# Spectral products by even and odd halves of the DFT tables, inside the projection's program, and attention's first stacks loaded early

## The reference, cut to what matters

```python
# x: (2, 8192, 512); 16 heads of 32; window W = 64
h   = layernorm(x)
qkv = h @ w_qkv                                  # 512 -> 1536
out_local  = softmax over the keys from 32 before to 31 after each query, times v
out_global = softmax over every 64th key, times v
x = x + layernorm((out_local + out_global) @ w_out + b_out)
# spectral layer, w = w_freq_real + i*w_freq_imag, (512, 512)
y = real(ifft(fft(layernorm(x)) @ w)) + bias     # both over the last axis, 512
x = x + layernorm(y)
```

## Time and profile before

| | |
|---|---|
| median of 3 runs | 3774.73 us (3774.47 to 3777.2) |
| the profiled execution | 3778.02 us, of which the span is 3775.7 us |
| PE busy | 3697.7 us (98%) |
| DVE, POOL, ACT busy | 2319.9, 1928.3, 1587.6 us |
| projection, in the trace | start to 1125.5 us |
| spectral products | 1137.0 to 1223.6 us |
| attention | 1225.5 us to the end |

### The profile page before, as it was taken

The page is one execution under the profiler, slowest core; times in us unless marked ns, Lnnn a source line. Parts: engine busy times, 40 slices in busy tenths (PEclk is TensorE's granted clock), DMA queues, the critical chain, the costliest instruction groups (busy, mean ns, idle before and its releaser), DMA issues.

```text
span 3775.7 us, 77146 instructions
## 1 busy us (share of the span) xinstructions
PE 3697.7 (98%) x28480; PEld 2682.5 (71%) x28480; DVE 2319.9 (61%) x5331; ACT 1587.6 (42%) x3094; POOL 1928.3 (51%) x3087
## 2 busy tenths in 40 slices
PE   8999999999999899999999999999999999999997
PEld 6888888888874566666666666666666666666675
DVE  4333333333323567777777777777777777777774
ACT  3222222222220344555555555555555555555554
POOL 0000000000000367777777777777777777777777
PEclk9999999999999899999999999999999999999999
DMA  4554455445556456666666666666666666666651
GB/s 154 191 200 169 165 200 191 166 176 200 184 204 155 96 129 152 151 140 142 144 148 145 139 148 153 151 140 141 144 149 145 139 149 149 152 140 140 144 119 40
DMA packets 421938, 574.34 MB, mean 152 GB/s; under 512 B 41688, under 2 KB 186216, under 8 KB 421624
## 3 DMA queue, kind: packets, MB, share of 16 engines
q1 hardware_dynamic: 413080, 567.94, 57.1%
q10 hardware_dynamic: 8256, 2.16, 0.2%
q0 software_dynamic: 288, 0.08, 0.0%
HBM read 364.74 MB, written 203.23 MB: 150 GB/s over the span
## 4 chain that ended last, share of the span: by engine, by line
PE 62%; POOL 1%; ACTq 1%; ACT 0%; DVE 0%; issue 0%; POOLq 0%
PE ps_misc L995 19%; PE ps_max L915 10%; PE ps_sc L935 6%; PE ps_o L967 6%; PE ps_max L918 5%; PE ps_s L967 4%; PE ps_sc L949 4%; PE ps_o L979 3%; PE ps_s L973 3%; PE ps_sc L1004 1%; ACTq L782 1%; PE ps_sc L924 1%; PE ps_sc L943 1%; ACT qk L759 0%; POOL rsb L696 0%
## 5 line engine op out<-in xcount | busy, mean ns | idle before, releaser
L827 DVE TENSOR_REDUCE mx<-ps_max 128x2 f32<-128x256 f32 (+1 forms) x1365 | 485.0, 355 | 489.8 <-PE ps_max L918 466.7
L759 ACT ACTIVATE qk<-ps_sc 128x384 f32<-128x384 f32 (+1 forms) x1024 | 418.9, 461 | 666.0 <-PE ps_sc L935 663.3
L828 DVE TENSOR_REDUCE mx<-ps_max 128x2 f32<-128x384 f32 (+1 forms) x1365 | 612.6, 449 | 0.0
L915 PE MATMUL ps_max<-ks,qs 97*128 97x384 f32 x2048 | 569.1, 357 | 15.1 <-DVE mx L828 13.1
L915 PEld LDWEIGHTS ps_max<-ks,qs 97*128 97x128 f32 x2048 | 368.6, 192 | 180.9 <-DVE mx L828 127.1
L705 POOL TENSOR_SCALAR_AFFINE_SELECT qk<-qk 128x512 f32<-128x512 f32 (+1 forms) x512 | 298.5, 583 | 282.6 <-ACT qk L759 282.5
L371 PE MATMUL po<-ht_hi,w_hi 128*128 128x512 f32 x1024 | 405.6, 396 | 1.5 <-ACT ht_hi L248 1.5
L371 PE MATMUL po<-ht_hi,w_lo 128*128 128x512 f32 x1024 | 400.3, 391 | 0.0
L371 PE MATMUL po<-ht_lo,w_hi 128*128 128x512 f32 x1024 | 399.8, 390 | 0.0
L772 ACT ACTIVATE v<-ps_sc 128x512 f32<-128x512 f32 x512 | 298.2, 596 | 152.4 <-PE ps_sc L949 150.2
L918 PE MATMUL ps_max<-mask,ident_b 128*128 128x192 bf16 x2048 | 352.9, 254 | 0.0
(11 more groups left out here) (114 smaller groups left out, 7507.5 us busy)
## 6 DMA issues: line engine op xcount, KB each, us to landing
ks<-k_hi_d SPq DMA_DIRECT2D x256, 288.0 KB
qs<-q_hi_d SPq DMA_DIRECT2D x256, 256.0 KB
ks<-k_lo_d SPq DMA_DIRECT2D x128, 288.0 KB
xb<-in_L_attn_x SPq DMA_DIRECT2D x132, 256.0 KB, 3.5
q_lo_d<-o_lo SPq DMA_DIRECT2D x32, 1024.0 KB, 8.7
k_lo_d<-o_lo SPq DMA_DIRECT2D x32, 1024.0 KB, 10.1
qs<-q_lo_d SPq DMA_DIRECT2D x128, 256.0 KB
vw<-v_d SPq DMA_DIRECT2D x128, 256.0 KB, 2.9
```

What stands on the lines that cost most here:

```text
L759: nc.scalar.activation(p_loc[:, i, 2 * hp:2 * hp + 2, lo:MW], ps_sc[n % 2][:, 0:2 * MW].rearrange("p (h n) -> p h n", h=2)[:, :, lo:MW], A ...
L827: nc.vector.tensor_reduce(mx[s % 2][:, 1, h:h + n, tile], ps_max[:, b:b + n, MW:MW + NGLOB], axis=AX.X, op=ALU.max)
L828: last = nc.vector.tensor_reduce(mx[s % 2][:, 0, h:h + n, tile], ps_max[:, b:b + n, 0:MW], axis=AX.X, op=ALU.max)
L915: nc.tensor.matmul(ps_max[:, b, 0:2 * MW], qs[g][0:ROWS_MAX, h, tile * P:(tile + 1) * P], both_keys(g, h, tile), start=True, stop=True)
```

## The change

The separate spectral program is gone: its work stands at the end of the projection's block, after each engine's last chunk. There is one barrier less.

The tables are two now, cos and sin, and each product uses only half of a table: 257 columns of cos (the part that is even in the column's index) and 255 of sin (the odd part). A tile needs 4 matmuls of 128x257 and 4 of 128x255, in two PSUM banks, where it had 8 of 128x512 in one. ACT copies the odd half out of PSUM, and DVE (`mirrored`) makes the full 512 columns with three instructions: left half as sum or difference, right half with reversed columns, and two single columns. The scale 1/512 is an ACT instruction on M instead of being in a table. The loop over tiles has steps 1 and 2 interleaved, on all 8 banks (`pt` and `po`).

The stacks lie in the projection's freed buffers (`w_both` is w_hi and w_lo in one; `low` is `o_lo0`). Groups 0 and 1 (`EARLY = 2`) are loaded in the first block, groups 2 and 3 at the start of attention, between the loads of the values. The memsets of groups 2 and 3's key rows go to POOL there. b_out and b_ffn are loaded in attention, w_out in the last chunk. `s_t` shares `r_glob`'s buffer. The mask and the bf16 identity are loaded at the program's start.

```diff
-    return np.stack([c, s, c / D, -s / D]).astype(np.float32)
+    return np.stack([np.cos(angle), np.sin(angle)]).astype(np.float32)
...
 # project_phase, sync: load_spectral, called ahead of the last chunk's stores
-                    sp.dma_start(v0[:], rows(dft_d[0])).then_inc(spec_loaded, 16)
-                    for k in range(2):
-                        sp.dma_start(qk0[:, k * KT:(k + 1) * KT, :].bitcast(F32), rows(dft_d[1 + k])).then_inc(spec_loaded, 16)
+                    sp.dma_start(cos, rows(dft_d[0])[:, :, 0:EVEN]).then_inc(spec_loaded[0], 16)
+                    sp.dma_start(sin, rows(dft_d[1])[:, :, 1:ODD + 1]).then_inc(spec_loaded[0], 16)
+                    sp.dma_start(wo, rows(w_out)).then_inc(spec_loaded[1], 16)
+                    sp.wait_ge(kg_copied, 2 * NCHUNK)
+                    sp.dma_start(kg_hi_d.rearrange("(a p) n -> p a n", p=P), kg_hi[:].bitcast(F32)).then_inc(kg_stored, 16)
+                    sp.dma_start(kg_lo_d.rearrange("(a p) n -> p a n", p=P), kg_lo[:].bitcast(F32)).then_inc(kg_stored, 16)
...
 # behind the last chunk's stores
+                sp.wait_ge(kg_stored, 32)
+                sp.wait_ge(pads, 16 * PADS)
+                for g in range(EARLY):
+                    sp.wait_ge(stacks.q_made, g + 1)
+                    sp.wait_ge(stacks.k_made[g], 2)
+                    stacks.load(sp, 0, g)
+                for u in range(2):
+                    sp.wait_ge(stored[u], 16 * 5 * NCHUNK // 2)
...
 # scalar
+                act.wait_ge(spec_loaded[1], 16)
+                for k in range(KT):
+                    nc.scalar.activation(wo_hi[:, k, :], wo[:, k, :], ACT.Copy).then_inc(split_hi, 1)
+                act.wait_ge(row_made, 1)
+                for n in range(2 * KT):
+                    act.wait_ge(spec_mm, n + 1)
+                    nc.scalar.activation(odd[n % 2][:, n // 2, :], banks[(2 * n + 1) % 8][:, 0:ODD], ACT.Copy).then_inc(odd_copied, 1)
+                    if n in (1, 4):
+                        act.wait_ge(stacks.k_made[n // 4], 2)
+                        stacks.load_ones(act, n // 4)
+                for a in range(KT):
+                    act.wait_ge(spec_mm, 2 * KT + a + 1)
+                    nc.scalar.activation(odd[0][:, a, :], banks[2 * a + 1][:, 0:ODD], ACT.Copy).then_inc(odd_copied, 1)
+                    act.wait_ge(m_sum, 3 * a + 3)
+                    nc.scalar.activation(wr[:, a, :], wi[:, a, :], ACT.Copy, scale=1.0 / D).then_inc(m_scaled, 1)
+                    act.wait_ge(m_scaled, a + 1)
+                    nc.scalar.activation(m_hi[:, a, :], wr[:, a, :], ACT.Copy).then_inc(split_hi, 1)
...
 # vector
+                def mirrored(dst, even, odd, sign, done):
+                    plus, minus = (ALU.add, ALU.subtract) if sign > 0 else (ALU.subtract, ALU.add)
+                    half = D // 2
+                    nc.vector.tensor_tensor(dst[:, 1:half], even[:, 1:half], odd, plus).then_inc(done, 1)
+                    nc.vector.tensor_tensor(dst[:, half + 1:D], even[:, half - 1:0:-1], odd[:, ::-1], minus).then_inc(done, 1)
+                    nc.vector.tensor_copy(dst[:, 0:half + 1:half], even[:, 0:half + 1:half]).then_inc(done, 1)
+
+                dve.wait_ge(mm_done, NCHUNK * (NOUT + TILES))
+                stacks.set_queries(nc, 0)
+                stacks.set_keys(nc.vector, 0)
+                for a in range(KT):
+                    for n, dst in ((2 * a, at), (2 * a + 1, bt)):
+                        dve.wait_ge(odd_copied, n + 1)
+                        mirrored(dst[:, a, :], banks[2 * n % 8], odd[n % 2][:, a, :], 1 if dst is at else -1, spec_sum)
+                    if a == 0:
+                        stacks.set_queries(nc, 1)
+                        stacks.set_keys(nc.vector, 1)
+                    if a in (1, 2):
+                        stacks.set_queries(nc, a + 1)
...
+                for a in range(KT):
+                    dve.wait_ge(odd_copied, 2 * KT + a + 1)
+                    mirrored(wi[:, a, :], banks[2 * a], odd[0][:, a, :], -1, m_sum)
+                    if a > 0:
+                        low(a - 1)
+                low(KT - 1)
...
 # tensor
+                pe.wait_ge(spec_loaded[0], 16 * 4)
+                pe.wait_ge(t_lo, NCHUNK * TILES)
+                pe.wait_ge(ev_dve, NCHUNK * NOUT)
+                for n in range(2 * KT):
+                    a = n // 2
+                    if n == 2:
+                        pe.wait_ge(ev_act, NCHUNK * (NOUT + TILES))
+                    at_least(pe, spec_sum, 3, n, -9)
+                    even, odds = ((wr, wi), (wi, wr))[n % 2]
+                    product(banks[2 * n % 8], even, cos, a)
+                    product(banks[(2 * n + 1) % 8], odds, sin, a).then_inc(spec_mm, 1)
+                pe.wait_ge(spec_sum, 6 * KT)
+                for a in range(KT):
+                    product(banks[2 * a], at, cos, a)
+                    product(banks[2 * a + 1], bt, sin, a).then_inc(spec_mm, 1)
...
 # attention, sync
-                for g in range(GROUPS):
-                    load_values(0, g)
+                load_values(0, 0)
+                for g in range(EARLY, GROUPS):
+                    sp.wait_ge(stacks.k_made[g], 2)
+                    stacks.load(sp, 0, g)
+                    load_values(0, g - 1)
+                load_values(0, GROUPS - 1)
```

More of the change, by code:

```diff
@@ L67, in dft, with project_phase @@
     angle = 2.0 * np.pi * ((n[:, None] * n[None, :]) % D) / D
[L68 to L73 removed]
+    return np.stack([np.cos(angle), np.sin(angle)]).astype(np.float32)
+def project_phase(nc, x, w_qkv, q_hi_d, q_lo_d, k_hi_d, k_lo_d, v_d, kg_hi_d, kg_lo_d, bias_d, ident_d, mask_d,
+                  w_real, w_imag, dft_d, w_out, common, stacks):
     NOUT = 2 * KT
@@ L84, in project_phase @@
         kg_lo = sb("kg_lo", [P, KT, BATCH * NGLOB], F32R)
[L85 to L88, removed]
+        at, bt = sb("at", [P, KT, D], F32), sb("bt", [P, KT, D], F32)
+        wr, wi = xb
+        cos, sin, wo = v0[:, :, 0:EVEN], qk0[:, 0:KT, 0:ODD].bitcast(F32), qk0[:, KT:2 * KT, :].bitcast(F32)
+        odd = v0[:, :, EVEN:EVEN + ODD], qk0[:, 0:KT, ODD:2 * ODD].bitcast(F32)
+        m_hi, m_lo, wo_hi, wo_lo = ht_hi[1], ht_lo[1], ht_hi[0], ht_lo[0]
         w_raw = o_v[1]
@@ L385, in _, with product, __init__ @@
                 chunks(pe, body, first)
+                def product(bank, left, right, a):
+                    width = EVEN if right is cos else ODD
+                    for k in range(KT):
+                        last = nc.tensor.matmul(bank[:, 0:width], left[:, k, a * P:(a + 1) * P], right[:, k, :], start=k == 0, stop=k == KT - 1)
+                    return last
+                pe.wait_ge(spec_loaded[0], 16 * 4)
[13 more added lines that the diff above has]
+                    product(banks[2 * a + 1], bt, sin, a).then_inc(spec_mm, 1)
+class Common:
+    def __init__(self, nc, ctx):
+        sb = lambda n, s, d: ctx.enter_context(nc.sbuf_tensor(n, s, d))
+        self.xb = [sb(f"xb{u}", [P, TILES, D], F32) for u in range(2)]
+        self.v0 = sb("v0", [P, TILES, D], F32)
+        self.qk0 = sb("qk0", [P, 2 * KT, CHUNK], F32R)
+        self.ident = sb("ident", [P, P], F32)
+        self.ht_hi = [sb(f"ht_hi{u}", [P, KT, CHUNK], F32R) for u in range(2)]
+        self.ht_lo = [sb(f"ht_lo{u}", [P, KT, CHUNK], F32R) for u in range(2)]
+        self.w_both = sb("w_both", [P, 2 * KT * 3 * D], F32R)
+        half = KT * 3 * D
+        self.w_hi, self.w_lo = (self.w_both[:, i * half:(i + 1) * half].rearrange("p (k n) -> p k n", k=KT) for i in range(2))
+        self.low = sb("o_lo0", [P, 2 * KT * CHUNK], F32R)
+        self.o_lo0 = self.low[:].rearrange("p (k n) -> p k n", k=2 * KT)
 class Stacks:
-    def __init__(self, nc, ctx, ident, dram):
+    def __init__(self, nc, ctx, common, dram):
         sb = lambda n, s, d: ctx.enter_context(nc.sbuf_tensor(n, s, d))
@@ L538, in attention_phase @@
-def attention_phase(nc, x, v_d, m_hi, m_lo, wo_hi, wo_lo, xb, yb, p_glob, qk0, stacks, out):
+def attention_phase(nc, x, v_d, b_out, b_ffn, common, stacks, out):
     with ExitStack() as ctx:
@@ L689, in _ @@
             def _(pool):
+                for g in range(EARLY, GROUPS):
+                    stacks.set_keys(pool, g)
+                    pool.wait_ge(stacks.k_made[g], 2)
                 def rstd(k, c, i):
@@ L745, in _ @@
                 nc.scalar.preload_act_table_set("natural_log_exp_and_others")
+                for g in range(EARLY, GROUPS):
+                    act.wait_ge(stacks.k_made[g], 2)
+                    stacks.load_ones(act, g)
                 def norm(k, c, i, dst, src):
@@ L808, in _ @@
             def _(dve):
-                dve.wait_ge(stacks.const_loaded, CONST_LOADS)
                 def stats(k, c, i, src):
```

218 lines of the change are left out of this document (81 added, 137 removed).

## The result

The changed kernel takes 3728.99 us (median of 4 runs, 3725.7 to 3731.16, the profiled execution among them), the kernel before on the same chip 3775.97 us (4 runs, 3774.47 to 3780.58): ratio 0.9871, 95% interval 0.9856 to 0.9886, which is 47.0 us less. The forecast was 3724.2 with a range of 3716 to 3734. The profiled execution took 3731.16 us with a span of 3728.6, against 3778.02 and 3775.7, so the two traces differ by 46.9 to 47.1 us as well and can be read against each other.

A forecast was written before the change was run, and what follows sets the result against it. Attention was taken as bound by PE and its steady part as untouched; -11.6 - 2.9 - 38.9 + 0.5 + 1.9 + 0.5 = -50.5 us took the median from 3774.7 to 3724.2 us, range 3716 to 3734.

The forecast's parts named there:

- The barrier: Between projection and products: first product starts at 1125.40 instead of 1137.00 us, -11.6 us.
- the low clock behind the hole: First products after the idle gap: without the gap PE's clock does not fall, -2.9 us.
- Half-width products: Spectral products: 192 instructions of 257 and 255 columns at 0.227 us each, 43.5 instead of 82.4 us, -38.9 us.
- the narrow matmuls are not cheaper in full: Rival in the products: weight loads do not hide (3758 us) or width gains nothing (3763 us); chance 0.05.
- Who feeds the products: Products' tiles from n = 4: ACT and DVE free the banks in time, cover 7 us, cost nothing.
- Ahead of step 3: PE's idle before the products' step 3 grows from 0.88 to 1.4 us, +0.5 us.
- The end: Between the products and attention: PE's idle grows from 1.93 to 3.8 us, +1.9 us.
- Attention's start: Attention's first steps: clock at 0.5 from the start, about two max items slower, +0.5 us.
- The stacks: Stack loads before and early in attention: all land before PE asks, 13 us of cover for stack 1, all hidden.
- The stacks or tables come late: Rival at attention's start: loads sharing one queue with stores and values land after 1175 us, 3732 us; chance 0.06.
- the clock goes another way: Rival: clock falls at the step 3 hole or early attention, 3731 us, or falls less, 3718 us; chance 0.16.
- The slower case: Rival in attention: shared `s_t` and `r_glob` buffer lengthens each of 128 steps, 0.7 us each gives 3814 us; chance 0.02.

The follow-up runs named there:

- e9: The e3 kernel run again, on one chip with e8: changed kernel with stack 3 held back and mask and identity loads later; 3722.34 us.
- e3: Changed kernel with stack 3 and later loads held until step 0's row maxima landed, and mask and identity loads behind the first two norms; 3723.17 us.
- e1: Changed kernel with SP holding stack 3 and all loads behind it until step 0's row maxima have landed; 3724.97 us.
- e8: The e9 kernel plus four unread 384-column matmuls behind each row-maximum unit of attention's first two steps; 3717.65 us.

## Why the prediction was right, and where not

- **The barrier** (-11.6) and **the low clock behind the hole** (-2.9): right in place and size. The first product starts 0.23 us behind the projection at clock 1.00, and putting block and store order back costs 13.3 us, of which 11.6 are the hole. The cover was wider than forecast: cos and sin, issued at 1111.24 and 1111.65, landed 7.7 and 8.8 us later, 6 us or more before PE asked.
- **Half-width products** (-38.9): right in mechanism, mis-sized by 2.1. The pace is 0.2158 us, so 41.4 in all and -41.0 against 82.4. "I take this nearest row, 0.227" was the wrong end: that pace belongs to the projection's matmuls, and the width of the instruction at hand gave the time. The rival that the narrow matmuls are not cheaper in full is excluded by the same pace.
- **The loads.** By the Trainium skill ("TensorE: Matmul & The Clock Gate", "Part 3: Packing small matmuls") the 0.19 us loads would show, all being of the same rows. Here 192 loads cost nothing that can be seen, 1 ns each at most, so that rule, as the prediction used it, doesn't hold for this case. The same section also lets a load run ahead into a background weight buffer; no run here tells whether that is what happened.
- **Who feeds the products**: no wait for `spec_sum` in tiles 4 to 7. **Ahead of step 3**: 1.33 idle, forecast 1.4. **The end**: 3.90, forecast 3.8.
- **Attention's start** (+0.5): without the DMA wait, the way to the second transpose is 36.1 to 37.1 us (e9, e3, e1) against 36.3, so this lies between nothing and 0.8.
- **The stacks**: this step failed, and the sign that the prediction named for it, "if PE waits at attention's start for a DMA", came. "All hidden" was argued from when PE asks for each stack, and none was late. What was left out is that the same loads delay every small transfer on another queue that attention waits for at once. It cost PE 4.1 us, and 3.5 on the path; the traces of e1, e3 and e9 have 2.8 to 3.8 of them back. It is none of the rivals: "The stacks or tables come late" had the cause in SP's own queue.
- **The start-up**, which the prediction didn't speak of: the first product is 1.34 us later than by the sum, of which 0.9 stand already at the first transposes. **The end** of attention was 1.9 longer, but 82.9 to 85.7 in all kernels run here, so that is spread.

The sum by the measured sizes: -11.6 - 2.9 - 41.0 + 0.45 + 2.0 = -53.05 up to attention, with +1.34 from the start-up -51.7, as in the trace; then +3.5 - 0.8 + 1.9 gives -47.1. The forecast of -50.5 was 3.5 too large (the other 1.2 us between 3724.2 and 3728.99 are the kernel before, whose median became 3775.97): the missed wait (3.0 beyond the +0.5 forecast for attention's start), the start-up (1.3) and attention's steady part and end (1.1), less what the products gave beyond the forecast (2.1). That the errors partly cancel, and that the steady part came out within 0.8 us, is luck; the range of 3716 to 3734 had room for either.

The rival that the clock goes another way did not show at the two holes. Later in attention, every kernel has a low stretch some 100 to 125 us in, the changed one too (0.66 from 1280 to 1300 us, where the earlier trace rows have 0.61 from 1332), so the fall that the rival let drop out is still there. A second one, 40 to 105 us in, comes and goes: the kernel before has it (0.71 from 1280.5 to 1285.5), the changed kernel's profiled execution doesn't and its repeat does (0.50 from 1254.1 to 1259.1). The slower case is excluded: it needs 0.4 us a step, 50 us in all, and the 126 steps take 2429.2 against 2430.0 us.

## What to carry to other kernels

When bulk loads are moved into a stretch where the DMA engines were idle, look for every small transfer in that stretch on which an engine waits at once, on whichever queue it is. That the bulk itself is in time doesn't prove that nothing waits. One wait on the bulk queue, for the small transfer's own semaphore, was enough here. A barrier behind a store queue costs the issue of each store still ahead of it, so stores whose data is ready go first. And where matmuls get narrower, count them by their own columns before taking a pace from wider ones.

## What the hardware showed

- Two transfers of 8 KB on ACT's queue landed in 1.8 us with idle engines and in 9.0 us beside SP's stack and value loads at a DMA share of 1.1 (q1 110.0%, q10 1.7%); with stack 3 and the loads behind it held back, in 1.8 again. The Trainium skill ("DMA: Bandwidth & Descriptors", "Issuing engines are not separate DMA queues") says that ACT's and SP's queues feed the same 16 engines; the trace is in line with it, by these 9.0 us.
- Full fp32 matmuls of 257 and 255 columns run 0.2158 us apart with a load of 0.19 us each, 0.43 at 512 columns: the time goes with the columns down to here.
- DVE reads 255 columns backwards, one operand in PSUM and one in SBUF, as fast as forwards: 0.41 us for L394, 0.42 for L393.
- In attention's first steps PE was faster with more work: 144 matmul records at clock 0.89 took 29.4 us, 81 at 0.52 took 33.2 (profiled executions of e8 and e9).
